# Pooled blocks taken in pairs, and the carries' two matmul operands filled up with zeros from 8 to 128 partitions

## The reference

```python
# x: (2, 1024, 256); 8 experts and a shared one, each 256 -> 1024 -> 256
g = einsum('bsd,edf->ebsf', x, Wg); u = einsum('bsd,edf->ebsf', x, Wu)
expert_outs = einsum('ebsf,efd->ebsd', silu(g) * u, Wd)
x = x + (1 - sg) * einsum('be,ebsd->bsd', gating_probs, expert_outs) + sg * shared(x)

attn_in = tanh(x @ W1 + b1)              # (2, 1024, 64)
scores = attn_in @ v                     # (2, 1024)
# by the type of the batch entry: l <= j, l >= j, or l != j
masked = where(mask, scores[:, None, :], -1e30)
p = softmax(masked, axis=-1)             # (2, 1024, 1024)
cnt = sum(mask, axis=-1)
x = x + einsum('bjl,bld->bjd', p, x) / cnt[..., None]
```

## Time and profile before

| | us |
|---|---|
| median of 3 runs | 1155.12 |
| lowest and highest | 1150.12, 1157.04 |
| the profiled execution | 1155.26 |
| its span, first to last instruction | 1153.5 |

### The profile page before, as it was taken

How to read it: one execution, slowest core, us unless ns; L and a number is a source line. 1 busy time by engine, 2 the same in 40 slices (tenths; PEclk the granted TensorE clock), 3 DMA queues, 4 the chain that set the end, 5 groups by cost and what they waited for, 6 DMA issues and landing times.

```text
span 1153.5 us, 14918 instructions
## 1 busy us (share of the span) xinstructions
PE 1143.3 (99%) x4990; PEld 927.3 (80%) x4990; DVE 797.2 (69%) x1170; ACT 650.1 (56%) x1168; POOL 263.8 (23%) x349
## 2 busy tenths in 40 slices
PE   8999999999999999999999999999999999999998
PEld 5788888888888888888888888888888888877765
DVE  6977777766776776776666667766667777557654
ACT  5756655555555555555555555555555566446551
POOL 7511412132331212120202021212111144002100
PEclk9999999999999999999999999999999999999997
DMA  4100100000000000001000000000000011000002
GB/s 158 56 28 28 54 21 14 24 28 28 28 28 28 28 28 28 28 28 29 28 28 28 28 28 28 28 28 28 28 28 28 28 53 46 13 1 28 1 1 74
DMA packets 37932, 36.69 MB, mean 32 GB/s; under 512 B 3040, under 2 KB 37856, under 8 KB 37856
## 3 DMA queue, kind: packets, MB, share of 16 engines
q1 hardware_dynamic: 37040, 34.95, 9.7%
q10 hardware_dynamic: 816, 0.79, 0.2%
HBM read 33.63 MB, written 2.10 MB: 31 GB/s over the span
## 4 chain that ended last, share of the span: by engine, by line
PE 95%; DVE 1%; issue 0%; ACT 0%; DVEq 0%; ACTq 0%
PE acc L1003 11%; PE acc L1005 11%; PE acc L1004 11%; PE v_ps L1003 8%; PE v_ps L1005 8%; PE v_ps L1004 8%; PE e_ps L1005 5%; PE e_ps L1003 5%; PE e_ps L1004 5%; PE g_ps L1005 5%; PE g_ps L1003 5%; PE g_ps L1004 5%; PE acc L1132 0%; PE v_ps L1137 0%; PE v_ps L1132 0%; PE acc L1137 0%
## 5 line engine op out<-in xcount | busy, mean ns | idle before, releaser
L1003 PE MATMUL acc<-h_hi,wd_hi 128*128 128x512 f32 x576 | 225.2, 391 | 0.0
L1004 PE MATMUL acc<-h_hi,wd_lo 128*128 128x512 f32 x576 | 224.2, 389 | 0.0
L1005 PE MATMUL acc<-h_lo,wd_hi 128*128 128x512 f32 x576 | 224.2, 389 | 0.0
L567 ACT ACTIVATE silu<-g_ps 128x512 f32<-128x512 f32 x144 | 86.1, 598 | 225.1 <-PE g_ps L1005 225.1
L561 ACT ACTIVATE v_ps<-g_ps 128x512 f32<-128x512 f32 x144 | 84.0, 583 | 189.7 <-PE g_ps L1005 189.7
L808 DVE TENSOR_TENSOR gate<-e_ps,v_part 128x512 f32<-128x512 f32 x144 | 99.5, 691 | 122.6 <-PE e_ps L1005 122.2
L826 DVE SCALAR_TENSOR_TENSOR v_ps<-silu,gates,v_ps 128x512 f32<-128x512 f32 x144 | 108.7, 755 | 93.0 <-PE v_ps L1005 91.7
L1003 PE MATMUL v_ps<-xs_hi,wq_hi 128*128 128x512 f32 x432 | 168.8, 391 | 1.4 <-DVE up L813 1.2
L1005 PE MATMUL v_ps<-xs_lo,wq_hi 128*128 128x512 f32 x432 | 168.3, 390 | 0.0
L1004 PE MATMUL v_ps<-xs_hi,wq_lo 128*128 128x512 f32 x432 | 168.3, 390 | 0.0
L431 POOL TENSOR_TENSOR wd_hi<-raw_d,zero 128x256 fp32r<-128x256 f32 x80 | 55.5, 693 | 423.0 <-PE acc L1005 421.1
(11 more groups left out here) (169 smaller groups left out, 1913.6 us busy)
## 6 DMA issues: line engine op xcount, KB each, us to landing
raw_d<-in_L_cond_Wd SPq DMA_DIRECT2D x35, 256.0 KB, 3.7
raw<-in_L_cond_Wg SPq DMA_DIRECT2D x34, 256.0 KB, 2.6
raw<-in_L_cond_Wu SPq DMA_DIRECT2D x34, 256.0 KB, 3.2
out_x<-x_nat SPq DMA_DIRECT2D x8, 256.0 KB, 2.1
x_nat<-in_x SPq DMA_DIRECT2D x7, 256.0 KB, 5.5
raw<-in_L_cond_Sg SPq DMA_DIRECT2D x5, 256.0 KB, 2.6
raw<-in_L_cond_Su SPq DMA_DIRECT2D x5, 256.0 KB, 2.9
raw_d<-in_L_cond_Sd SPq DMA_DIRECT2D x5, 256.0 KB, 3.6
```

The lines of the kernel that those rows point to most:

```text
L567: nc.scalar.activation(silu0[:, i % 2, :], g_ps[:], ACT.Silu).then_inc(silu0_done, 1)
L1003: nc.tensor.matmul(ps, w_hi, a_hi, start=start, stop=False, skip_group_check=True)
L1004: nc.tensor.matmul(ps, w_lo, a_hi, start=False, stop=False, skip_group_check=True)
L1005: return nc.tensor.matmul(ps, w_hi, a_lo, start=False, stop=stop, skip_group_check=True)
```

## The change

`blk_sum` and `carry` get 128 partitions in place of 8. ScalarE still writes the first 8 of each; the others stay at zero, which three memsets provide: of `blk_sum` by GpSimd among the constants, of `carry[0]` by VectorE at the end of group `L1_AT`, and of `carry[1]` by GpSimd after the last product of batch entry 1. A new semaphore `carry_zeroed` holds ScalarE's first writes to `carry` until these are done. `pooled` is not changed, but its carry matmuls now take all 128 partitions, so they feed 128 rows of the array. In addition, batch 0's blocks are taken two at a time, as batch 1's are.

```diff
-        blk_sum = sb("blk_sum", [NJ, B, D + 1])
+        blk_sum = sb("blk_sum", [P, B, D + 1])
...
-            carry.append(place(f"carry{b}", [NJ, S], F32, at))
+            carry.append(place(f"carry{b}", [P, S], F32, at))
...
+        carry_zeroed = sem("carry_zeroed")
...
-        CONST_STEPS = 2 + 2 + 1 + 1 + 1 + 1 + 6 + 3 + 3 + B * (2 + 4 + 6 + 3)
+        CONST_STEPS = 1 + 2 + 2 + 1 + 1 + 1 + 1 + 6 + 3 + 3 + B * (2 + 4 + 6 + 3)
...
+
+                const(nc.gpsimd.memset(blk_sum[:], 0.0))
                 const(nc.gpsimd.tensor_scalar(neg_eye[:], ident[0:NJ, 0:NJ], -1.0, None, ALU.mult))
...
                 nc.gpsimd.memset(x1[b][:, :, D:XA], 1.0).then_inc(x1_ones, 1)
+                if b:
+                    pool.wait_ge(carry_zeroed, b)
+                    nc.gpsimd.memset(carry[b][:], 0.0).then_inc(carry_zeroed, 1)
...
                 act.wait_ge(max_done, n + 1)
-                nc.scalar.activation(carry[0][:, n * BANK:(n + 1) * BANK], MAXB[0][n][0:NJ, :],
+                act.wait_ge(carry_zeroed, 1)
+                nc.scalar.activation(carry[0][0:NJ, n * BANK:(n + 1) * BANK], MAXB[0][n][0:NJ, :],
...
                 act.wait_ge(sum_done, b + 1)
-                nc.scalar.activation(blk_sum[:, b, :], SUM[b], ACT.Copy).then_inc(sum_copied, 1)
+                act.wait_ge(const_step, CONST_STEPS)
+                nc.scalar.activation(blk_sum[0:NJ, b, :], SUM[b], ACT.Copy).then_inc(sum_copied, 1)
...
                 act.wait_ge(dve_l1, DVE_L1["bias", b])
+                act.wait_ge(carry_zeroed, b + 1)
...
-                    nc.scalar.activation(carry[b][:, j * P:(j + 1) * P], src, ACT.Exp,
+                    nc.scalar.activation(carry[b][0:NJ, j * P:(j + 1) * P], src, ACT.Exp,
...
-                if k == 1:
+                if k == 0:
+                    dve.wait_ge(p_done[3], end_of_b[0] + 1)
+                    nc.vector.memset(carry[0][:], 0.0).then_inc(carry_zeroed, 1)
+                elif k == 1:
...
-            pooled(0, range(len(POOLED)))
+            for j in range(0, len(POOLED), HEAD):
+                pooled(0, range(j, j + HEAD))
             block_sums(1, range(NJ))
-            pooled(0, range(len(POOLED), NJ))
+            for j in range(len(POOLED), NJ, HEAD):
+                pooled(0, range(j, j + HEAD))
```

More of the change, by code:

```diff
@@ L626, in copy_sum @@
                 act.wait_ge(sum_done, b + 1)
-                nc.scalar.activation(blk_sum[:, b, :], SUM[b], ACT.Copy).then_inc(sum_copied, 1)
+                act.wait_ge(const_step, CONST_STEPS)
+                nc.scalar.activation(blk_sum[0:NJ, b, :], SUM[b], ACT.Copy).then_inc(sum_copied, 1)
             def exp_carry(b, blocks):
                 act.wait_ge(dve_l1, DVE_L1["bias", b])
+                act.wait_ge(carry_zeroed, b + 1)
                 for j in blocks:
                     n, at = j * P // BANK, slice(j * P % BANK, j * P % BANK + P)
-                    src = carry[b][:, j * P:(j + 1) * P]
+                    src = carry[b][0:NJ, j * P:(j + 1) * P]
                     if b == 0:
```

## The result

The changed kernel took 1148.17 us (median of 4 executions, 1147.94 to 1149.36). The kernel before took 1155.12 (1150.12 to 1157.04). The ratio is 0.993, 95% interval 0.9913 to 0.9947 (the two medians alone give 0.994). So it is faster by 0.5% to 0.9%, which the interval separates from no change, and within the 1% band that the prediction named likeliest. The forecast was 1147.6.

What follows compares the result with a forecast made beforehand. TensorE, busy 99% of the span and at half clock from 1137.2 us, was taken as the bound. 7.6 us of TensorE plus 0.1 of VectorE's tail, 7.7 off 1155.26, gave 1147.6 us; range 1145.5 to 1153.5.

Steps and rivals of the forecast that it cites:

- the 1% band: Whole kernel: time within 1% of 1155.12 us, that is 1143.6 to 1166.7 us; chance 0.92.
- The sum: TensorE from batch 0's first probabilities to batch 1's block 14: matmul times added up, ending 7.61 us earlier.
- Carries with 128 rows hold the clock: Carry matmuls at the end: added zero rows cost no time and count as work, so the clock stays at 1.00.
- the blank tile at the start: Kernel start: matmuls on an all-zero tile sped up from 0.46 to 0.29 us each, taken as zeros raising the clock.
- The shape changes: Probabilities and carries at the end: one common shape hides weight loads, saving 0.19 us at each former change.
- the semaphore waits: Ahead of the first carries: alternative reading that 0.33 us idle comes from waits at each pair, not from shape.
- last rival: End of kernel: in most runs the clock does not fall; also 1147.6 us, gain 1.8 us, inside the forecast's 0.60.
- Pairs and memsets: Batch 0's order adds no matmuls and costs nothing; the three memsets fit in idle time, nothing to 0.1 us.
- The clock falls as before: Rival, end of kernel: clock drops at 1137.2 us despite the filled rows; 1152 to 1156.4 us, chance 0.20.
- falls earlier: Rival: clock drops already at the first carry, 1125.26 us, giving 1167.6 us; chance 0.06 for 1156 to 1168.
- pieces still cost: Rival, end of kernel: clock stays, but each two-block matmul group after the first takes 1.06 us; 1150.2 us, chance 0.14.

Runs made afterwards that it cites:

- the 96-row kernel: The changed kernel with carry matmuls that read 96 partitions instead of 128: 1149.75 us median of 4.
- the filled-up kernel: The changed kernel with neg_max and ones also filled to 128 rows and e_diag to 128 columns: 1147.25 us, in its second measurement 1148.78 us.

## Why the prediction was right

**The sum.** Predicted from the first probabilities piece to block 14: 7.61 us less; measured 7.64. VectorE's work behind it was forecast at some 1.65 us and is 1.68 (1143.12 to 1144.80), and the last store again takes 2.5 (to 1147.3).

**Carries with 128 rows hold the clock.** Right in effect: eight rows alone, with everything else of the change kept, gave the median of before and the low clocks of before. In the traces, the 8-row kernel before has a fall among the carries and the kernels with 16 rows or more have none. Where the falls of the other 8-row executions stood is not shown. That zeros count held too: rows filled with zeros held the clock, and ones in the moving operand changed nothing. The prediction drew it from the blank tile at the start, and there it went by durations. The granted clock reads 1.00 in those stretches of the kernel before, although the matmuls took 0.46 us each and later 0.29:

```profile
2.00:3.00 1.00, 1.00 (x4) 0.71 (x4) 0.00 (x0) 0.62 (x1) 0.00 (x0) 1.00 0.68 147
```

So the column and the durations disagree ahead of the first fall at 14 us, and the start alone did not prove the step; the filled carries do. The reason that I gave, few rows fed, was right only in direction. Carries of 32 rows hold the clock as well as 128, and 16 did in the one trace there is, which a share of the array would not explain.

**The shape changes.** Right, at 0.19 us each, also where the clock stayed high with eight rows. Of the two readings that the prediction weighed, the shape and the semaphore waits, the 96-row kernel decides for the shape: it has all the waits and none of the idle time. With the changes of shape gone, weight loads of one shape are hidden (pieces of 0.87 us), as the prediction read from its rows and against the Trainium skill's rule on row groups (TensorE: Matmul & The Clock Gate, Part 3, "What overlaps and what doesn't").

**How the gain divides.** The kernel before without a fall at its end is near 1150, by its own lowest of 1150.12 (whose clock is not on record) and by the prediction's estimate of 1149.4. So about 5 of the 7 us are the clock and about 2 the shapes, an estimate, since no trace shows that kernel without the fall. The prediction's sum held both, and its last rival put the shapes at 1.8.

**Pairs and memsets.** Right that they cost nothing: VectorE's memset took 0.91 us (0.96 forecast) inside 3.03 us of idle time, GpSimd's took 0.53 and 0.95, inside the bounds. The pairs' use of 0.28 us (no bank wait in batch 1's first pair) is in the prediction's sum, which takes that piece at 0.87 where it was 1.15, but it was not put down to the pairs.

**The missing half microsecond.** 1148.17 is 0.57 above 1147.6. Executions of the changed kernel spend 2.05 us outside their span, against 1.76 before, which is 0.3; where that comes from was not looked into. The other 0.27 is too little for a fall in mid kernel, which costs 1.5. Where it comes from stays open. It is within the scatter of the traces that have no fall but the early one between 13 and 18 us: there the first piece starts anywhere from 1124.11 to 1124.70.

**What the prediction had wrong.** It read the level of 1.00 between 1113.9 and 1120.4 as a sign that narrow columns do not cost the clock. In that one trace it is so. But the clock fell between 1118 and 1122 in two experiments (16 rows, and the filled-up kernel in its second measurement), and behind batch 0's score columns, between 1036 and 1042, in four traces. That the score columns cause these falls is suggested by the place, and not shown.

**The rivals.** "The clock falls as before" and "falls earlier" did not happen in any of the 10 executions of the changed kernel, by their mean clocks of 0.996 to 0.999, and by both traces. The last rival, that in most executions of the kernel before the clock does not fall, is out by the 33 later executions of it, none above 0.994. The time of "pieces still cost" is what 32 and 64 rows show (forecast 1150.2, measured 1150.76 and 1150.44), though by changes of shape and not by waits.

## What to carry to other kernels

Look at the granted clock in stretches, not only in the mean: 0.991 over the whole execution was 0.50 from 1137.2 to 1149.9, a stretch where TensorE was never idle. If matmuls that feed a few rows alternate there with full ones, filling their operands up with zeros costs TensorE nothing in time, needs one memset where an engine idles, and can bring back both the clock and the weight loads' cover. For the cover 96 rows were enough here and 64 were not; for the clock 32 were enough. With falls that come and go between executions, compare many executions with their clocks, look in the trace where each fall stood, and take the chain of waits of an execution without a fall for the price of everything else.

## What the runs showed of the hardware that was not expected

- The clock can fall while TensorE is busy without a gap (11.20 of 11.20 us up to the fall at 1137.2). With carries of 8 rows, 33 later executions of the kernel before had mean clocks of 0.988 to 0.994, and nine of ten of the 8-row experiment 0.987 to 0.995; with 32 or 64 rows all ten had 0.998. What it is about 8 rows as against 32 stays open.
- It also falls for some 3 us in mid kernel, behind the score columns (16 records of 64x1 in 1.9 us), in some executions and not in others of the same kernel. Such a fall costs about 1.5 us: 1149.36 with it, 1147.94 to 1148.30 without. No kernel here was made to remove it.
- The early fall costs about 2 us or nothing, by where it stands: in the 64-row trace at 22 us, in the 32-row trace at 14 us, with a mean clock of 0.998 in both.
- A change between a shape of 8 to 64 rows and the full array costs 0.19 us; between 96 and 128 rows, nothing.
